# Attention scores of two heads issued together as 64-row products, with keys packed like the queries

## What is computed

```python
q = (x @ Wq + bq).reshape(B, S, N_HEAD, HEAD_DIM).transpose(0, 2, 1, 3)
k = (x @ Wk + bk).reshape(B, S, N_HEAD, HEAD_DIM).transpose(0, 2, 1, 3)
...
scores = jnp.einsum('bhqd,bhkd->bhqk', q / math.sqrt(HEAD_DIM), k)
scores = scores + attention_bias
scores = jnp.where(src_mask, -jnp.inf, scores.astype(jnp.float32))
probs = jax.nn.softmax(scores, axis=-1).astype(v.dtype)
ctx = jnp.einsum('bhqk,bhkd->bhqd', probs, v)
```

## Time and profile before

| | |
|---|---|
| median of 3 runs | 970.0 us (968.17 to 973.71) |
| the profiled execution | 967.02 us |
| its span, first to last instruction | 964.9 us |
| mean granted TensorE clock | 0.960 |
| PE, DVE, ACT, POOL busy | 88%, 77%, 64%, 15% of the span |

### The profile page before, as it was taken

One profiled execution on the slowest core, in us unless ns is written; L12 is line 12 of the kernel. 1 busy time (PEld: TensorE's weight loads), 2 busy tenths in 40 slices (PEclk: granted clock), 3 DMA queues, 4 the chain that ended last, 5 costly groups with the idle time before them and its releaser, 6 DMA issues.

```text
span 964.9 us, 18444 instructions
## 1 busy us (share of the span) xinstructions
PE 845.6 (88%) x5962; PEld 711.9 (74%) x5962; DVE 744.3 (77%) x2457; ACT 613.8 (64%) x1247; POOL 146.1 (15%) x144
## 2 busy tenths in 40 slices
PE   2375989899999999899999999998999999898884
PEld 0254768788878888788888888887888888787772
DVE  3558676696979787897969797878979697959465
ACT  1133767676867676767768676767677686666320
POOL 2111011111111111111111111111111111101010
PEclk9587899999999999999999999999999999999987
DMA  6624546455464635454554746364555546452100
GB/s 200 204 73 128 166 153 173 139 160 162 141 176 131 175 130 137 158 160 157 160 167 140 176 126 180 111 174 137 168 156 161 161 129 164 140 153 80 50 22 22
DMA packets 147734, 137.56 MB, mean 143 GB/s; under 512 B 19298, under 2 KB 144803, under 8 KB 147636
## 3 DMA queue, kind: packets, MB, share of 16 engines
q1 hardware_dynamic: 147636, 136.33, 47.9%
HBM read 98.49 MB, written 4.23 MB: 106 GB/s over the span
## 4 chain that ended last, share of the span: by engine, by line
PE 68%; DVE 17%; SPq 5%; issue 5%; ACT 2%; DMA 2%; POOL 0%; POOLq 0%; DVEq 0%; ACTq 0%
PE back_bank L1030 10%; PE turn_bank L986 8%; PE front_bank L1055 6%; PE front_bank L1024 5%; PE score_bank L1088 5%; PE context_bank L1040 5%; PE score_bank L1089 4%; PE back_bank L1024 4%; PE attend_bank L1024 4%; DVE sc L819 3%; DVE fN L774 3%; PE back_bank L1010 3%; PE front_bank L1194 3%; PE back_bank L1001 3%; PE attend_bank L1010 3%
## 5 line engine op out<-in xcount | busy, mean ns | idle before, releaser
L819 DVE CUSTOM_DVE_ANT_0 sc<-score_bank,side 128x256 f32<-128x256 f32 x512 | 195.4, 419 | 95.7 <-PE score_bank L1089 89.6
L519 ACT ACTIVATE sc<-sc,negmax 128x256 f32<-128x256 f32 x512 | 230.0, 499 | 23.6 <-DVE negmax L819 22.9
L505 ACT ACTIVATE pt<-turn_bank 128x512 f32<-128x512 f32 x176 | 104.8, 595 | 178.1 <-PE turn_bank L986 146.1
L986 PE MATMUL turn_bank<-ident,sc 128*128 128x128 f32 x1024 | 157.8, 277 | 1.7 <-ACT sc L519 1.5
L986 PEld LDWEIGHTS turn_bank<-ident,sc 128*128 128x128 f32 x1024 | 124.7, 142 | 36.2 <-issue 14.3
L447 POOL TENSOR_TENSOR rstd<-var,half_neg 128x2 f32<-128x2 f32 x64 | 49.4, 772 | 638.9 <-DVE var L753 638.9
L1088 PE MATMUL score_bank<-ks,qs 128*128 128x256 f32 x512 | 122.6, 321 | 7.0 <-DVE negmax L819 6.5
L1030 PE MATMUL back_bank<-w,ffT 128*128 128x256 f32 x512 | 118.0, 379 | 0.0
L1030 PEld LDWEIGHTS back_bank<-w,ffT 128*128 128x128 f32 x512 | 97.0, 190 | 12.6
L1089 PE MATMUL score_bank<-mask_neg,ident_r 128*128 128x512 f32 x256 | 102.1, 399 | 0.0
L1088 PEld LDWEIGHTS score_bank<-ks,qs 128*128 128x128 f32 x512 | 78.4, 193 | 15.5 <-DVE negmax L819 8.2
(11 more groups left out here) (199 smaller groups left out, 1901.7 us busy)
## 6 DMA issues: line engine op xcount, KB each, us to landing
side<-in_side SPq DMA_DIRECT2D x128, 512.0 KB, 4.9
qs<-qh SPq DMA_DIRECT2D x128, 64.0 KB, 2.6
ks<-kh SPq DMA_DIRECT2D x128, 64.0 KB, 2.6
ks<-kl SPq DMA_DIRECT2D x128, 64.0 KB, 2.6
qs<-ql SPq DMA_DIRECT2D x128, 64.0 KB, 2.6
wb<-in_wb SPq DMA_DIRECT2D x16, 512.0 KB, 3.9
xN<-in_x SPq DMA_DIRECT2D x16, 256.0 KB, 4.0
ada<-ada_rows SPq DMA_DIRECT2D x16, 256.0 KB, 5.3
```

The source lines that it names most:

```text
L505: e.activation(pt[:, h % NP2, :, :], two(tbank[h % 2]), ACT.Copy).then_inc(copied[h % 4], 1)
L519: i = e.activation(sc[:, h % NS, q, :], sc[:, h % NS, q, :], ACT.Exp, bias=negmax[:, q, h:h + 1], scale=-1.0)
L819: i = e.tensor_tensor_reduce(sc[:, s % NS, q, :], two(sbank[s % 2])[:, q, :], side[:, (H * X.i + s) % NSIDE, q, :], -1.0, 3.4e38, ALU.add, ...
L986: i = e.transpose(tbank[h % 2][:, k * S + q * P:k * S + q * P + P], sc[:, h % NS, q, k * P:k * P + P], ident[:, :])
```

## The change

The keys are packed in pairs like the queries, so `ks` has 8 slots in place of 16, and the zeros and their memset are gone (with one increment of `ready` less, which SET0 counts). Scores are issued in even steps only, for heads s and s + 1: four products over 64 partitions, alternating between the lower half (head s, bank 0) and the upper half (head s + 1, bank 1), and behind them the two mask products over all partitions. Both heads' banks must be free first.

```diff
@@ stack (SP)
-                        e.dma_start(ks[to, HM * m + u:HM * m + HM:2, :].bitcast(F32), k_[at, m, :].bitcast(F32)).then_inc(ld_stack[m], 16)
+                        e.dma_start(ks[to, HU * m:HU * m + HU, :].bitcast(F32), k_[at, m, :].bitcast(F32)).then_inc(ld_stack[m], 16)
@@ GpSimd, before the turns
-            e.memset(ks[:, :, :].bitcast(F32), 0.0).then_inc(ready, 1)
@@ PE, body
-                    if X:
+                    if X and s % 2 == 0:
                         if s % HM == 0:
                             e.wait_ge(ld_stack[s // HM], times(X, STACKED))
-                        head(e, biased, X, s - 2)
                         if s == 0:
                             e.wait_ge(ev["mask_ready"], X.n)
+                        for u in range(2):
+                            head(e, biased, X, s + u - 2)
                         for q in range(TT):
-                            e.matmul(two(sbank[s % 2])[:, q, :], qs[:, s // 2, q * P:q * P + P], ks[:, s, :], start=(q == 0), stop=False)
-                        i = e.matmul(sbank[s % 2][:, :], ident_r[:, :], mask_neg[:, X.par, :, :], start=False, stop=True)
-                        i.then_inc(scored[s % 4], 1)
+                            for u in range(2):
+                                e.matmul(two(sbank[u])[:, q, :], qs[64 * u:64 * u + 64, s // 2, q * P:q * P + P], ks[64 * u:64 * u + 64, s // 2, :],
+                                         start=(q == 0), stop=False)
+                        for u in range(2):
+                            e.matmul(sbank[u][:, :], ident_r[:, :], mask_neg[:, X.par, :, :], start=False, stop=True).then_inc(scored[(s + u) % 4], 1)
```

More of the change, by code:

```diff
@@ L41 @@
 LT = 2
-SET0 = 2
+SET0 = 1
 ACT_COPIES = (0, 1, 2, 3, 4, 7, 8, 9, 13, 14, 15)
@@ L162, in build @@
         qs = sb("qs", [P, H // 2, S], F32R)
-        ks = sb("ks", [P, H, S], F32R)
+        ks = sb("ks", [P, H // 2, S], F32R)
         mask_raw = sb("mask_raw", [P, TT, S // 4], I32)
```

## The result

The changed kernel takes 991.6 us (median of 4 runs, 986.9 to 993.4), the kernel before beside it 969.1 (4 runs, 966.9 to 973.7): a ratio of 1.022, 95% interval 1.017 to 1.027, so it is slower. The profiled execution took 992.8 us.

A forecast was written before the change was run, and what follows sets the result against it. A PE-DVE loop sets the 53.0 us batch; 0.55 + 0.09 + 0.26 - 0.10 + 0.14 = 0.94 us a batch, 11.3 over twelve, plus 1 at the ends, on 967.0 gives 979.3, plus 3.0 for the median 982.3; range 965 to 999.

The forecast's parts named there:

- the loop: PE from step 0 to wo in step 8, then DVE from x2 to head 15's bias; sets the 53 us batch.
- the serial rival: Score products: the two halves run one after the other; 2.12 us a batch, 996 us with shape changes; chance 0.20.
- the wait at step 0: PE idles 0.63 us at step 0 because the scores now wait for head 15's bias.
- the 0.50 more ahead of wo: Step 8: pair (8,9) now stands whole ahead of wo, which comes 0.50 us later.
- the 0.36 that DVE no longer waits for head 9: DVE's 0.36 us wait for head 9's scores goes, leaving 0.14 of the 0.50 ahead of wo.
- the round trip: PE's shape change around a pair's score products: 0.26 us (ends 0 and 0.35), making a pair 0.03 dearer.
- The stretch from step 0 to head 4's bias: Pairs (0,1), (2,3) cost 0.03 us each, bias 4 comes 0.26 later; the way in (0.08) hides at step 0.
- -0.28 + 4.7R: Batch growth in us for a round trip R; below R = 0.06 the batch gets shorter.
- step 5: Head 5's products leave step 5; only 0.10 of their 0.47 us is won, since the branch stands there.
- 0.94: Predicted growth of one batch in us, from step 0 to the next, all terms together.
- The ends: First and last batches, which lack stages: 1 us added in all, between 0 and 3.
- the rival built on that: Score products: change of shape (nearly) free; 968 us, or 963 with all of step 5 won; chance 0.15.

The follow-up runs named there:

- full-height pairs: Kernel before with the scores of two heads issued together in even steps, its own keys and 128-row products kept: 979.7 us, ratio 1.0126.
- early load: Load of wb issued at step 0, ahead of the sixteen stacking transfers: kernel before 961.3 us, ratio 0.9911; changed kernel 990.3 us.
- moved scores: Kernel before with head 5's scores moved ahead of the wait for t_e in step 4: 971.9 us, ratio 1.0015; with wb's load also issued earlier 962.3.
- single heads: Changed kernel with packed keys and 64-row products, but issued one head a step: 1040.1 us, ratio 1.0765.
- second visit: Changed kernel with its mask products cut in two halves, the first two placed between the two rounds of products: 1038.3 us in one run.

## Why the prediction was right

The direction, the two causes and the loop were right, and the time lies in the range. But the forecast was 12.3 us of loss and 22.5 were measured, and the forecast's own bounds, 978 to 988, were missed: it was the wide range, held open for the serial rival, that took the time in.

**Right: the direction, and the wait at step 0.** 0.63 us a batch were predicted there and 0.64 measured, both with and without half-height products. So were the 0.50 more ahead of wo (0.53), the 0.36 that DVE no longer waits for head 9 (0.38), nothing from head 9's to head 15's bias (20.09 and 20.08), and that the halves overlap.

**Off in size: the round trip.** I took 0.26 us from the context strips; it measured 0.39, above the 0.35 that I gave as the upper end. A pair of heads costs 0.15 more than before, not 0.03. What I missed is that the change of shape is paid twice at each edge, once at the first operation and once at the second. The stretch from step 0 to head 4's bias was to grow by 0.24 and grew by 0.47. The trace splits it: the first product of pair (4,5) comes 0.26 later, behind two whole pairs (0.30, less 0.06 that full-height pairs win there, since head 3 no longer stands behind the context products); head 4's mask another 0.11; and its end 0.10 more. By my own formula, -0.28 + 4.7R, 0.39 would have given 1.55 a batch against the 1.10 measured. Half of the difference is that it charged a whole round trip ahead of a pair's first mask, where a part lies behind, and ahead of wo, where the way in had been paid before the cut; the other half is step 5, below. So that 0.94 came near 1.10 is partly luck: too small a round trip, charged in too many places.

**Off in cause: step 5.** I gave its stretch -0.10 and laid the rest to the branch. Ahead of the products with wb it came to -0.43. The early load alone, which leaves the branch as it was, shortens this stretch by 0.21 in the kernel before: that part was the transfer. Behind them stand +0.21 and +0.06 for step 6's pair and the way in at step 8. The three stretches together are -0.16, where I had -0.10 and +0.03.

**Not foreseen and of no weight: the wait for vp.** Head 9's scores used to fill it. It lies in PE's slack ahead of n3l; n3l's wait, which was to stay about as long, falls from 1.75 to 1.19 us and doesn't run out.

**The sum.** 1.10 a batch against 0.94; the first biases of batches 3 and 15 stand 12 batches and 649.5 us apart instead of 635.4, +14.2 against the predicted 11.3 (the last of the twelve alone lost 2.1). The ends: from the first bias to that of batch 3 +4.1 us, behind batch 15's +2.3, where I had 1 in all. PE's wait for the bias in the first batches, 6.5 us in the earlier trace rows, is 14.6 now in 60 to 168 us, and 17.6 with full-height pairs. So the pairing makes it, not the shape; that a pair must wait for both heads' banks where DVE is behind is the likely reason, but I ran nothing that shows it. The last 5.4 us of the span lie ahead of the first bias (66.2 and 71.6 us). They don't look like the change's, as it came at 65.8 in the changed kernel with the early load and at 72.0 in the kernel before with the moved scores. So the 991.6 came closer to the 996 of the serial halves than that rival deserves: its mechanism is refuted, and the batch of 54.14 is not its 55.1.

The Trainium skill, "TensorEngine Tiling (Array Packing)", Key Properties, says that changing the tiling mode drains TensorE. The trace agrees that a change costs something, 0.39 us a round trip; whether by a drain it doesn't show. The Trainium skill, "TensorE: Matmul & The Clock Gate", Part 3, counts packed products as one product and some 4 ns for each further tile. Inside a round the trace agrees, with starts 3 to 4 ns apart; but it names no cost of going in and out, and the rival built on that falls with the 0.39 us.

## What to carry to other kernels

Two half-height products run in the time of one, but that pays only inside a long visit to that shape. Here a round saves 0.12 us and a round trip costs 0.39, so by my estimate a visit must hold at least four rounds before it pays, and it held two; no run had four rounds of useful work. Before work is grouped, ask on which loop the first of the group will now wait for the last of the one before; that cost a little more than the changes of shape did (0.62 and 0.48 us a batch). And when a gap in front of an operation is labelled "issue", compare it with the issue time of each transfer it reads, over all batches: a constant shortest distance points to a transfer, and issuing that one earlier tests it.

## What the runs showed of the hardware

- A change between 128-row and 64-row fp32r products costs PE 0.09 us before the first operation and 0.10 before the second, in both directions: 0.39 a round trip with single heads, and 0.42 for a second visit. Behind four turns of 128 columns the way in falls as 0.17 and 0.02. Behind the context products (18 columns) it adds 0.01 to what the way out of those costs anyway.
- A round of two half-height products takes 0.12 us, as one full-height product does; the two start 3 to 4 ns apart.
- The order in which products of the two halves are issued made no difference (0.51 and 0.50 us for four).
- A 64-row weight load of 128 columns takes as long as one of 128 rows (190 against 193 ns, the means of the changed kernel's two lines): height saves nothing there.
- The first product with a transfer of 0.5 MB started 4.53 us after its issue at the earliest; ahead of it, sixteen small ones kept SyncE's queue for 11 us.
